# Delta attention on one Trainium2 core: block products placed in pairs on two halves of the PSUM partitions, output scaling moved to ScalarE

## The chip, the cores and the metric

The kernel runs on one core of one Trainium2 chip. The core has TensorE (PE, with its weight loads listed as PEld), VectorE (DVE), ScalarE (ACT), GpSimd (POOL) and SyncE (SP), which issues the DMAs. They run side by side and meet only through semaphores. The metric is the device time of one execution in microseconds, the median of several runs.

## The reference, cut to what matters

Input x is 4 x 1024 x 128. Four layers are added to it in turn: a gated delta-rule attention (8 heads, three delta updates in each step), a mixture of 15 experts, a decay attention and the mixture again. Only the first is touched by the change. For each head it computes, in sequence over t:

```python
q, k, v = short_conv(x @ Wq), short_conv(x @ Wk), short_conv(x @ Wv)   # 4 taps, then silu
def step(S, inp):
    S = S * exp(g_t)
    for i in range(3):
        S = S + beta_i * k_i (v_i - k_i S)       # outer product
    return S, q_t S
o = o * rsqrt(mean(o * o) + 1e-5) * rms_weight   # over the 128 columns of a head
o = (o * silu(x @ Wg)) @ Wo
```

## The kernel before, in words

`delta_attention` cuts time into chunks of 32 steps. With three updates a step, a chunk has R = 96 rows. An iteration takes SPAN = 64 steps (two chunks, `cc` 0 and 1) of all four sequences of one head, so it has U = 8 units (sequence, chunk), in two halves of HU = 4. There are 8 heads x 16 = 128 iterations' worth of work. The loop variable f runs over 142 rounds, and each round holds three stages of different chunks at once:

- the k side of iteration f: `k_tile` projects x to k and q (TensorE, lines 1100 and following), `tap0` on ScalarE (L766) and `tap1` to `tap3` on VectorE (L931) do the convolution, `ksilu` and `qsilu` on ScalarE (L798, L807) the silu. For iteration f - 1: `ktr` transposes (L1151), `ksum_` squares and sums on ScalarE (L730), `kr` scales (L738), `gram` makes k k' (L1163), `ap` masks it (L960, L964).
- the c side, iteration c = f - 11: `v_tile` and `gate_tile` (L1100), the v taps, `vsilu` (L781), `gate_` (L788), `vtr` and `vr` (L1173, L971), and the merge of the block inverses. The 96 x 96 unit-triangular system of a chunk is inverted in three diagonal blocks of 32 x 32 by GpSimd (`subst`, L701 and L704, four iterations together). Then `zm` (L1182), `wm` (L1191) and `m3` (L1199) on TensorE make the off-diagonal blocks for the eight units in PSUM tensor ZW, and `zev` (L822, L823), `w12` (L829) and `yev` (L835) on ScalarE copy them out to Zt and Yf.
- the recurrence of iteration r = f - 12 in two steps: `ks` (L1054), `rhs_` (DVE L879), `w_` (L1064), `wev` (ACT L756), `sr` (L1074), `sup` (DVE L890), and `o_` (L1089, L1090) for the output. `fo_` on GpSimd (L678, L680) makes the factor of the RMS norm, `osb_` (DVE L978) multiplies by it, `ot` transposes (L1207), `og_` (L986) gates, `out` (L1214) projects, `acc_` (L994) adds to x.

Each engine's order of work in a round is written out by hand as a list of calls at the end of its block. No engine leaves its order; a wait in one call holds all behind it. PSUM tile PP has two buffers, which tiles v0, v2, k0, k2 and v1, gate, k1, q share in turn, so a projection waits until VectorE has finished the taps of the one before it in the same buffer: for `gate_tile`

```python
need(pe, taps_ev[1], N)
```

that is the third tap of v1. Every fourth round ScalarE begins with `xt` (L841), a transposing copy of the finished diagonal blocks. `o_` already writes its four sequences' results to four groups of 32 PSUM partitions:

```python
o = o_ps[b * TC:(b + 1) * TC, cc, :]
mm(o, kqgB[N % 2][:, u, R:128], S[cc][:, b, :], start=True, stop=False)
```

A float32 matmul of the program appears as two matmuls and two weight loads in the trace, so eight units are 16.

Of the kernel before, what the change touches and what calls it, by code (L numbers as in the profile page):

```python
# [16 lines left out]
ALU = mybir.AluOpType  # L17
ACT = mybir.ActivationFunctionType
AX = mybir.AxisListType

B, T, D = 4, 1024, 128
# [3 lines left out]
R = NHH * TC  # L25
NCC = 2
SPAN = NCC * TC
U = B * NCC
KSTEPS = T // SPAN
PAD = TAPS - 1  # L30
HU = U // 2
TILE = 512
# [51 lines left out]
def need(eng, sem, n):  # L84

    if n >= 0:
        eng.wait_ge(sem, n + 1)
# [272 lines left out]
def delta_attention(nc, g):  # L360
# [7 lines left out]
    BLK = R // NHH  # L368
    with ExitStack() as ctx:
        new_sem = semaphores(nc, ctx)  # L370
        sb = lambda n, s, dt=F32: ctx.enter_context(nc.sbuf_tensor(n, s, dt))
        two = lambda n, s: [sb(f"{n}{i}", s) for i in range(2)]
# [34 lines left out]

        kqgB = two("kqgB", [128, U, 128])
        recB = two("recB", [R, U * 128 + U * TC])
        apkB, Dd = two("apkB", [64, U, 64]), two("Dd", [64, U, 64])  # L410
        Yf = two("Yf", [R, U, R])
        Zt = sb("Zt", [R, U, 64])
        vt = sb("vt", [128, U, R])
# [8 lines left out]

        pb = lambda n, s: ctx.enter_context(nc.psum_tensor(n, s, F32))
        PP, TG = [pb(f"PP{i}", [128, TILE]) for i in range(2)], pb("TG", [128, U, 128])
        ZW, RA, RB, SD = pb("ZW", [128, U, 64]), pb("RA", [128, B, 128]), pb("RB", [128, B, 128]), pb("SD", [128, TILE])
        o_ps, ot_ps = SD[:, 0:256].rearrange("p (c n) -> p c n", c=NCC), SD[:, 256:512]

        kqg_d = nc.dram_tensor("kqg_d", (SETS * KSTEPS, 128, U * 128), F32, kind="Internal").ap()
# [26 lines left out]
        def live(n):  # L455
            return 0 <= n < NS
# [4 lines left out]
        def slot(n):  # L461
            return (n // KSTEPS) % SETS * KSTEPS + n % KSTEPS
# [12 lines left out]

        def half(t, hf):
            return t[:, hf * HU:(hf + 1) * HU]

        def of_cc(t, cc):
            return t.rearrange("p (b c) n -> p b c n", c=NCC)[:, :, cc, :]  # L480
# [27 lines left out]
        def _(sp):  # L508
# [63 lines left out]
            def da_load(N):  # L572
                if not live(N):
                    return
                q = N // GROUP
                need(sp, zm_mm, N - 2)
                sp.wait_ge(preset_ev, 1)
                sp.wait_ge(st_ap[N % 2], 4 * uses(N))
                sp.dma_start(apkB[N % 2][:, :, :], apk_d[slot(N)]).then_inc(ld_da[N % 2], 16)
                sp.wait_ge(st_x[q % 2], uses(q))  # L580
                for b in range(2):
                    o = slice(BLK * b, BLK * (b + 1))
                    sp.dma_start(Dd[N % 2][o, :, o], x_d[q, lanes(N, b)].rearrange("u r c -> r u c")).then_inc(ld_da[N % 2], 16)
# [48 lines left out]
        def _(pool):  # L632
# [70 lines left out]
                    x = X[q % 2][:, j + 1:, 0:cols]  # L703
                    nc.gpsimd.tensor_tensor(x, x, t, ALU.subtract).then_inc(sub_ev, 1)  # L704

            for t in (Zt, Yf[0], Yf[1], Dd[0], Dd[1]):
                nc.gpsimd.memset(t[:, :, :], 0.0)
            nc.gpsimd.memset(S[0][:, :, :], 0.0).then_inc(preset_ev, 1)
            for f in range(NF):
# [11 lines left out]
        def _(act):  # L721
            def ksum_(N, hf):
                if not live(N):
                    return
                need(act, ktr_mm[hf], N)
                need(act, ss_ev, N - 1)
                if N >= 2:
                    act.wait_ge(st_rec[N % 2], uses(N - 2))
                for u in units_of(hf):
                    last = nc.scalar.activation(recA[N % 2][:, u * 128:(u + 1) * 128], TG[:, u, :], ACT.Square, accum_out=ksum[:, u:u + 1])  # L730
                last.then_inc(ksum_ev[hf], 1)
# [26 lines left out]
            def tap0(N, name):  # L758
                if not live(N):
                    return  # L760
                i, x = TILES[name], N // KSTEPS % 2
                src = PP[i % 2][:, 0:B * (PAD + SPAN)].rearrange("p (b t) -> p b t", b=B)
                need(act, tile_mm[i], N)
                need(act, vsilu_ev if i < 3 else qsilu_ev if i == 7 else ksilu_ev, N - 1)
                acc, w = (conv_v[:, i], tv[x][:, i, 0:1]) if i < 3 else (conv_k[:, i - 4], tk[x][:, i - 4, 0:1])
                nc.scalar.activation(acc, src[:, :, 0:SPAN], ACT.Copy, scale=w).then_inc(tap0_ev[i], 1)  # L766
# [42 lines left out]
            def mo_(N, cc):  # L809
# [3 lines left out]
                need(act, fs_ev, N - 1)  # L813
                nc.scalar.activation(osq[:, :], o_ps[:, cc, :], ACT.Square, accum_out=mo[:, cc:cc + 1]).then_inc(mo_ev[cc], 1)

            def zev(N):
                if not live(N):
                    return
                need(act, zm_mm, N)
                need(act, m3_mm, N - 1)  # L820
                act.wait_ge(preset_ev, 1)
                nc.scalar.activation(Zt[32:64, :, 0:32], ZW[0:32, :, 0:32], ACT.Copy, scale=-1.0)  # L822
                nc.scalar.activation(Zt[64:96, :, :], ZW[32:64, :, :], ACT.Copy, scale=-1.0).then_inc(zev_ev, 1)  # L823

            def w12(N):
                if not live(N):
                    return
                need(act, wm_mm, N)
                nc.scalar.activation(Yf[N % 2][32:64, :, 64:96], ZW[32:64, :, 32:64], ACT.Copy).then_inc(w12_ev, 1)  # L829

            def yev(N):
                if not live(N):
                    return
                need(act, m3_mm, N)
                nc.scalar.activation(Yf[N % 2][0:32, :, 32:96], ZW[0:32, :, :], ACT.Copy).then_inc(yev_ev, 1)  # L835

            def xt(q, k):
                if q is None or k:
# [4 lines left out]
            for f in range(NF):  # L843
                r, c = f - BACK - 1, f - BACK
                xt(*group_at(f, 2 * GROUP + 1))
                tap0(c, "v0")
                tap0(c, "v1")
                ksum_(f - 1, 1)
                ksum_(f - 1, 0)
                wev(r, 0)  # L850
                tap0(c, "v2")
                gate_(c)
                zev(c)
                tap0(f, "k1")
                mo_(r, 0)
                tap0(f, "k0")
                kr(f - 1, 0)
                vsilu(c)
                kr(f - 1, 1)
                tap0(f, "k2")  # L860
                w12(c)
                wev(r, 1)
                q2_(f - 1)
                tap0(f, "q")
                mo_(r, 1)
                yev(c)
                ksilu(f)
                qsilu(f)

        @block.vector  # L870
        def _(dve):
# [98 lines left out]
                need(dve, rk_ev, N)  # L970
                nc.vector.tensor_tensor(half(vrow[N % 2][:, :, :], hf), half(TG[0:R, :, :], hf), half(rk[:, N % RING, :], hf).unsqueeze(2).broadcast_to([R, HU, 128]), ALU.mult).then_inc(vr_ev[hf], 1)  # L971

            def osb_(N):
                if not live(N):
                    return
                need(dve, fo_ev, N)
                need(dve, ot_mm, N - 1)
                nc.vector.tensor_tensor(osb[:, :, :], o_ps, fo[:, :].unsqueeze(2).broadcast_to([128, NCC, 128]), ALU.mult).then_inc(osb_ev, 1)  # L978

            def og_(N):  # L980
                if not live(N):
                    return
# [15 lines left out]
            for f in range(NF):  # L998
                r, c = f - BACK - 1, f - BACK
                tap1(c, "v0")  # L1000
                osb_(r - 1)
                tap2(c, "v0")
                rhs_(r, 0)
                tap3(c, "v0")
                tap1(c, "v1")
                og_(r - 1)
                tap2(c, "v1")
                tap3(c, "v1")
                ss_(f - 1)
                rinv_(f - 1)  # L1010
                acc_(r - 1)
                tap1(c, "v2")
                step_(f - 1)
                tap2(c, "v2")
                tap3(c, "v2")
                sup(r, 0)
                es_(f - 1)
                tap1(f, "k1")
                tap1(f, "k0")
                tap2(f, "k0")  # L1020
                tap3(f, "k0")
                rhs_(r, 1)
                tap2(f, "k1")
                ap(f - 1, 0)
                tap3(f, "k1")
                tap1(f, "k2")
                tap2(f, "k2")
                ap(f - 1, 1)
                tap3(f, "k2")
                tap1(f, "q")  # L1030
                tap2(f, "q")
                tap3(f, "q")
                vr(c, 1)
                sup(r, 1)
                vr(c, 0)

        @block.tensor
        def _(pe):
# [137 lines left out]
            def zm(N):  # L1176
                if not live(N):
                    return
                pe.wait_ge(ld_da[N % 2], 3 * uses(N))
                need(pe, yev_ev, N - 1)  # L1180
                for u in range(U):
                    last = mm(ZW[0:64, u, :], apkB[N % 2][:, u, :], Dd[N % 2][:, u, :], start=True, stop=True)  # L1182
                last.then_inc(zm_mm, 1)

            def wm(N):
                if not live(N):
                    return
                need(pe, zev_ev, N)
                pe.wait_ge(ld_y[N % 2], 3 * uses(N))
                for u in range(U):  # L1190
                    last = mm(ZW[0:64, u, :], Zt[:, u, :], Yf[N % 2][:, u, BLK:R], start=True, stop=True)  # L1191
                last.then_inc(wm_mm, 1)

            def m3(N):
                if not live(N):
                    return
                need(pe, w12_ev, N)
                for u in range(U):
                    last = mm(ZW[0:32, u, 32:64], Zt[:, u, 0:32], Yf[N % 2][:, u, 64:96], start=True, stop=True)  # L1199
                last.then_inc(m3_mm, 1)  # L1200

            def ot(N):
# [837 lines left out]
```

## Time and profile before

| | |
|---|---|
| median of 3 runs | 3191.56 us (3190.16 to 3193.73) |
| the profiled execution's own time | 3186.49 us |
| its span | 3184.4 us |
| delta attention | from 72 us to about 2467 us of the span |
| busy share of the span | PE 94%, PEld 74%, DVE 79%, ACT 71%, POOL 62% |
| mean busy share of the DMA engines between 300 and 2310 us | 0.71 |

A row of the timeline gives the start in us, the time taken by the instructions merged into it, engine, line, operation, out<-in, shapes and count, and in brackets idle time before it with what ended it. Matmuls and weight loads overlap, so the row of 16 matmuls lasts from the first start to the last end. A row of waits gives the total in us, the number of times and the longest. A row of one source line gives the shortest, median and longest duration in ns, and the first and last start.

### The profile page before, as it was taken

Reading aid. Unit: us, or ns where it says so; the run is one execution under the profiler, and the core shown is the slowest. Engines: PE = TensorE matmul, PEld = TensorE weight load, DVE = VectorE, ACT = ScalarE, POOL = GpSimd, SP = SyncE. Lnnn points to the kernel's source line nnn. Section 1 sums busy time; section 2 is a strip of 40 time slices with the busy share of each in tenths; the row PEclk is TensorE's granted clock in tenths of the full one; section 3 lists DMA queues with packets and bytes.
Section 4 is the critical chain, followed back from the end, with each engine's and each line's share of the span. In section 5 each row is a group of like instructions: output and inputs, shape, how many; then the busy total and the mean of one; then the engine's idle time right before and its main releaser. Section 6 shows DMA issues by size and latency. Waiting matters only on the chain. (4 is left out here: it accounts for less than half of the span.)

```text
span 3184.4 us, 83423 instructions
## 1 busy us (share of the span) xinstructions
PE 2986.1 (94%) x27212; PEld 2356.1 (74%) x27212; DVE 2530.9 (79%) x5859; ACT 2250.1 (71%) x6955; POOL 1977.0 (62%) x3125
## 2 busy tenths in 40 slices
PE   5669999999999999999999999999988999867999
PEld 3458888888888888888888888888877444455444
DVE  5669999999999999999999999999855445585544
ACT  4768888888888888888888888888743444314443
POOL 1588888888888888888888888888851000100000
PEclk8779999999999999999999999999999899968999
DMA  5456777776767776767777767676732333002242
GB/s 108 121 154 167 191 180 182 172 181 170 181 172 189 177 178 174 185 167 182 174 185 178 185 171 178 176 180 168 184 96 64 129 148 130 30 3 73 108 160 113
DMA packets 588203, 482.87 MB, mean 152 GB/s; under 512 B 464784, under 2 KB 504368, under 8 KB 581632
## 3 DMA queue, kind: packets, MB, share of 16 engines
q1 hardware_dynamic: 579328, 474.39, 56.5%
q8 instruction: 223, 3.65, 0.5%
q10 hardware_dynamic: 8448, 3.15, 0.4%
q14 instruction: 204, 1.67, 0.2%
HBM read 285.53 MB, written 191.86 MB: 150 GB/s over the span
## 5 line engine op out<-in xcount | busy, mean ns | idle before, releaser
L931 DVE SCALAR_TENSOR_TENSOR conv_k<-PP,tk,conv_k 128x256 f32<-128x256 f32 x1536 | 722.7, 479 | 60.0 <-ACT conv_k L766 32.8
L704 POOL TENSOR_TENSOR X<-X,tmp 96x31 f32<-96x31 f32 (+15 forms) x992 | 534.8, 539 | 77.8
L931 DVE SCALAR_TENSOR_TENSOR conv_v<-PP,tv,conv_v 128x256 f32<-128x256 f32 x1152 | 539.3, 477 | 44.9 <-ACT conv_v L766 35.3
L701 POOL TENSOR_TENSOR tmp<-At,X 96x31 f32<-96x31 f32 (+15 forms) x992 | 486.3, 490 | 63.3 <-DMA At<-n_d 5.0
L1100 PE MATMUL PP<-xn,wk 128*128 128x268 f32 x1024 | 342.3, 418 | 38.0 <-DVE conv_k L931 26.3
L687 POOL TENSOR_TENSOR rk<-ss,half 96x8 f32<-96x8 f32 x128 | 209.1, 1634 | 175.2 <-DVE ss L899 175.2
L669 POOL TENSOR_TENSOR Sg<-S,gend 128x512 f32<-128x512 f32 x256 | 265.9, 1039 | 59.2 <-DVE S L890 59.2
L738 ACT ACTIVATE recA<-TG,es 96x128 f32<-96x128 f32 x1024 | 284.9, 368 | 5.1 <-DVE es L924 5.1
L766 ACT ACTIVATE conv_k<-PP,tk 128x256 f32<-128x256 f32 x512 | 245.3, 480 | 57.1 <-PE PP L1100 49.7
L730 ACT ACTIVATE recA<-TG 128x128 f32<-128x128 f32 x1024 | 265.5, 272 | 25.5 <-PE TG L1151 25.5
L1064 PE MATMUL RB<-rhs,Yf 96*96 96x128 f32 x2048 | 269.0, 274 | 14.5 <-DVE rhs L879 14.3
L756 ACT ACTIVATE ws<-RB 96x512 f32<-96x512 f32 x256 | 151.7, 592 | 183.0 <-PE RB L1064 180.1
L1054 PE MATMUL RA<-S,kqgB 128*96 128x128 f32 x2048 | 276.2, 278 | 1.0 <-DVE S L890 1.0
L1074 PE MATMUL RA<-ws,recB 96*128 96x128 f32 x2048 | 270.9, 275 | 0.2 <-ACT ws L756 0.2
L1064 PEld LDWEIGHTS RB<-rhs,Yf 96*96 96x96 f32 x2048 | 242.2, 163 | 36.9 <-DVE rhs L879 24.5
L1074 PEld LDWEIGHTS RA<-ws,recB 96*128 96x128 f32 x2048 | 259.0, 192 | 8.1 <-ACT ws L756 0.8
L1163 PE MATMUL TG<-kq 128*96 128x128 f32 x1888 | 245.3, 273 | 1.2 <-ACT recA L738 1.0
L1054 PEld LDWEIGHTS RA<-S,kqgB 128*96 128x96 f32 x2048 | 233.4, 163 | 13.0 <-DVE S L890 4.4
L654 POOL TENSOR_TENSOR kqgA<-kq,gdec 128x768 f32<-128x768 f32 x128 | 203.2, 1588 | 38.3 <-ACT kq L807 31.5
L1163 PEld LDWEIGHTS TG<-kq 128*96 128x96 f32 x1888 | 219.0, 163 | 2.2 <-ACT recA L738 2.2
L1100 PE MATMUL PP<-xn,wv 128*128 128x268 f32 x768 | 218.3, 391 | 2.3 <-DVE conv_k L931 2.3
L1100 PEld LDWEIGHTS PP<-xn,wk 128*128 128x128 f32 x1024 | 161.6, 197 | 69.5 <-issue 37.7
(291 smaller groups left out, 6735.0 us busy)
## 6 DMA issues: line engine op xcount, KB each, us to landing
kqg_d<-kqgA SPq DMA_DIRECT2D x128, 512.0 KB, 6.4
kqgB<-kqg_d SPq DMA_DIRECT2D x128, 512.0 KB, 4.5
rec_d<-recA SPq DMA_DIRECT2D x128, 480.0 KB, 3.4
recB<-rec_d SPq DMA_DIRECT2D x128, 480.0 KB, 6.0
f1gates<-f1gates_d SPq DMA_DIRECT2D x24, 1024.0 KB, 6.5
f2gates<-f2gates_d SPq DMA_DIRECT2D x24, 1024.0 KB, 6.8
gdec<-gdec_d SPq DMA_DIRECT2D x128, 128.0 KB, 5.8
apk_d<-apkA SPq DMA_DIRECT2D x128, 128.0 KB, 3.3
```

Of the source, the lines that this page charges most:

```text
L669: nc.gpsimd.tensor_tensor(Sg[:, :, :], S[cc][:, :, :], d.broadcast_to([128, B, 128]), ALU.mult).then_inc(sg_ev[cc], 1)
L701: nc.gpsimd.tensor_tensor(t, At[q % 2][:, j, j + 1:].unsqueeze(2).broadcast_to(sh), X[q % 2][:, j, 0:cols].unsqueeze(1).broadcast_to(sh), ...
L704: nc.gpsimd.tensor_tensor(x, x, t, ALU.subtract).then_inc(sub_ev, 1)
L730: last = nc.scalar.activation(recA[N % 2][:, u * 128:(u + 1) * 128], TG[:, u, :], ACT.Square, accum_out=ksum[:, u:u + 1])
L738: last = nc.scalar.activation(recA[N % 2][0:R, u * 128:(u + 1) * 128], TG[0:R, u, :], ACT.Copy, scale=es[:, u, TC - 1:TC])
L766: nc.scalar.activation(acc, src[:, :, 0:SPAN], ACT.Copy, scale=w).then_inc(tap0_ev[i], 1)
L931: return nc.vector.scalar_tensor_tensor(acc, src[:, :, j:j + SPAN], w[:, j:j + 1], acc, ALU.mult, ALU.add)
L1054: last = mm(RA[0:R, b, :], kqgB[N % 2][:, b * NCC + cc, 0:R], S[cc][:, b, :], start=True, stop=True)
L1064: last = mm(RB[0:R, b, :], Yf[N % 2][:, b * NCC + cc, :], rhs[:, b, :], start=True, stop=True)
L1074: last = mm(RA[:, b, :], recB[N % 2][:, u * 128:(u + 1) * 128], ws[cc][:, b, :], start=True, stop=True)
L1100: mm(out, w, x, start=True, stop=True).then_inc(tile_mm[i], 1)
L1163: last = mm(gram_bank(N, hf)[0:R, u % HU, :], kq[N % 2][:, u, 0:R], kq[N % 2][:, u, :], start=True, stop=True)
```

## The change

- `zm`, `wm` and `m3` write the products of units 0 to 3 to PSUM partitions 0 to 63 and those of units 4 to 7 to partitions 64 to 127 of ZW, which is half as long, and go through the units in the order 0, 4, 1, 5, 2, 6, 3, 7.
- apkB and Dd have 96 partitions in place of 64, the last 32 are zero, so `zm` contracts over 96 rows. GpSimd clears apkB too at the start. `m3` takes all 64 columns of Zt as weights in place of 32.
- `zev`, `w12` and `yev` take two copies, one from each half, where they took one: 4, 2 and 2 instructions in place of 2, 1 and 1.
- `osb_` moves from VectorE (one instruction over both chunks, after `tap1` of v0) to ScalarE (one Copy with a scale for each chunk, after `tap0` of v1 and ahead of `ksum_`).

```diff
-        apkB, Dd = two("apkB", [64, U, 64]), two("Dd", [64, U, 64])
+        apkB, Dd = two("apkB", [R, U, 64]), two("Dd", [R, U, 64])
-        ZW, RA, RB, SD = pb("ZW", [128, U, 64]), ...
+        ZW, RA, RB, SD = pb("ZW", [128, HU, 64]), ...
+        def paired():
+            return (HU * p + i for i in range(HU) for p in range(2))
+        def spot(u, lo, hi):
+            return ZW[64 * (u // HU):64 * (u // HU) + 64, u % HU, lo:hi]
-            for t in (Zt, Yf[0], Yf[1], Dd[0], Dd[1]):
+            for t in (Zt, Yf[0], Yf[1], Dd[0], Dd[1], apkB[0], apkB[1]):
                 nc.gpsimd.memset(t[:, :, :], 0.0)
...
+            def osb_(N):                      # ScalarE
+                need(act, fo_ev, N)
+                need(act, ot_mm, N - 1)
+                for cc in range(NCC):
+                    last = nc.scalar.activation(osb[:, cc, :], o_ps[:, cc, :], ACT.Copy, scale=fo[:, cc:cc + 1])
+                last.then_inc(osb_ev, 1)
             def zev(N):
-                nc.scalar.activation(Zt[32:64, :, 0:32], ZW[0:32, :, 0:32], ACT.Copy, scale=-1.0)
-                nc.scalar.activation(Zt[64:96, :, :], ZW[32:64, :, :], ACT.Copy, scale=-1.0).then_inc(zev_ev, 1)
+                for p in range(2):
+                    nc.scalar.activation(half(Zt[32:64, :, 0:32], p), ZW[64 * p:64 * p + 32, :, 0:32], ACT.Copy, scale=-1.0)
+                    last = nc.scalar.activation(half(Zt[64:96, :, :], p), ZW[64 * p + 32:64 * p + 64, :, :], ACT.Copy, scale=-1.0)
+                last.then_inc(zev_ev, 1)
             def w12(N):
-                nc.scalar.activation(Yf[N % 2][32:64, :, 64:96], ZW[32:64, :, 32:64], ACT.Copy).then_inc(w12_ev, 1)
+                for p in range(2):
+                    last = nc.scalar.activation(half(Yf[N % 2][32:64, :, 64:96], p), ZW[64 * p + 32:64 * p + 64, :, 32:64], ACT.Copy)
+                last.then_inc(w12_ev, 1)
             def yev(N):
-                nc.scalar.activation(Yf[N % 2][0:32, :, 32:96], ZW[0:32, :, :], ACT.Copy).then_inc(yev_ev, 1)
+                for p in range(2):
+                    last = nc.scalar.activation(half(Yf[N % 2][0:32, :, 32:96], p), ZW[64 * p:64 * p + 32, :, :], ACT.Copy)
+                last.then_inc(yev_ev, 1)
...
                 tap0(c, "v1")
+                osb_(r - 1)
                 ksum_(f - 1, 1)
...
-            def osb_(N):                      # VectorE
-                nc.vector.tensor_tensor(osb[:, :, :], o_ps, fo[:, :].unsqueeze(2).broadcast_to([128, NCC, 128]), ALU.mult).then_inc(osb_ev, 1)
                 tap1(c, "v0")
-                osb_(r - 1)
                 tap2(c, "v0")
...
-                for u in range(U):
-                    last = mm(ZW[0:64, u, :], apkB[N % 2][:, u, :], Dd[N % 2][:, u, :], start=True, stop=True)
+                for u in paired():
+                    last = mm(spot(u, 0, 64), apkB[N % 2][:, u, :], Dd[N % 2][:, u, :], start=True, stop=True)
...
-                for u in range(U):
-                    last = mm(ZW[0:64, u, :], Zt[:, u, :], Yf[N % 2][:, u, BLK:R], start=True, stop=True)
+                for u in paired():
+                    last = mm(spot(u, 0, 64), Zt[:, u, :], Yf[N % 2][:, u, BLK:R], start=True, stop=True)
...
-                for u in range(U):
-                    last = mm(ZW[0:32, u, 32:64], Zt[:, u, 0:32], Yf[N % 2][:, u, 64:96], start=True, stop=True)
+                for u in paired():
+                    last = mm(spot(u, 32, 64), Zt[:, u, :], Yf[N % 2][:, u, 64:96], start=True, stop=True)
```

## Rows read from the trace of the kernel before

**Rows 1.** Busy time of each engine between 300 and 2310 us (PE, PEld, DVE, ACT, POOL, clock, DMA).

```profile
300.00:2310.00 2010.00, 1999.97 (x20403) 1737.17 (x20400) 1842.20 (x4293) 1718.32 (x5558) 1704.50 (x2726) 1.00 0.71 178
```

**Rows 2.** Waits between 1000 and 2000 us: who for whom, total us, times, longest.

```profile
ACT ws L756 <- PE RB L1064: 58.9, 56, 1.2
...
PEld ZW L1191 <- issue: 19.9, 56, 0.4
...
DVE osb L978 <- POOL fo L680: 4.6, 14, 0.4
```

**Rows 3.** Timeline, ScalarE: the gate copy of three rounds in a row.

```profile
1489.65 0.38 ACT L788 ACTIVATE gate<-PP 128x256 f32<-128x256 f32 x1 [0.37 <-PE PP L1100]
...
1507.17 0.38 ACT L788 ACTIVATE gate<-PP 128x256 f32<-128x256 f32 x1 [0.37 <-PE PP L1100]
...
1525.44 0.38 ACT L788 ACTIVATE gate<-PP 128x256 f32<-128x256 f32 x1 [0.72 <-PE PP L1100]
```

**Rows 4.** Source line 822 up to 2312 us: one instruction a round.

```profile
L822 ACT ACTIVATE Zt<-ZW x119: 372/373/374, 216.4 to 2304.8; 32x256 f32<-32x256 f32 x119
```

**Rows 5.** Timeline, TensorE, one round.

```profile
1503.42 1.14 PE L1182 MATMUL ZW<-Dd,apkB 64*64 64x64 f32 x16
...
1508.41 0.45 PE L1089 MATMUL SD<-S,kqgB 128*32 128x128 f32 x8
1508.65 0.42 PE L1090 MATMUL SD<-ws,recB 96*32 96x128 f32 x8
...
1509.66 1.15 PE L1191 MATMUL ZW<-Yf,Zt 96*64 96x64 f32 x16
...
1512.56 0.62 PE L1100 MATMUL PP<-xn,wk 128*128 128x268 f32 x2
1513.02 1.04 PE L1064 MATMUL RB<-rhs,Yf 96*96 96x128 f32 x8
...
1514.77 0.62 PE L1100 MATMUL PP<-xn,wk 128*128 128x268 f32 x2
1515.32 0.45 PE L1089 MATMUL SD<-S,kqgB 128*32 128x128 f32 x8
...
1515.78 0.67 PE L1199 MATMUL ZW<-Yf,Zt 96*32 96x32 f32 x16
```

**Rows 6.** Timeline, ScalarE, the same round and the start of the next.

```profile
1507.58 0.37 ACT L822 ACTIVATE Zt<-ZW 32x256 f32<-32x256 f32 x1
1507.96 0.59 ACT L823 ACTIVATE Zt<-ZW 32x512 f32<-32x512 f32 x1
...
1514.76 0.84 ACT L747 ACTIVATE q<-ss 32x2 f32<-32x2 f32 x4
1515.62 0.47 ACT L766 ACTIVATE conv_k<-PP,tk 128x256 f32<-128x256 f32 x1
...
1518.36 2.01 ACT L841 ACTIVATE At<-X 96x1024 f32<-96x1024 f32 x1
...
1520.28 0.81 ACT L766 ACTIVATE conv_v<-PP,tv 128x256 f32<-128x256 f32 x2
```

**Rows 7.** Timeline, VectorE, end of that round and start of the next.

```profile
1510.28 1.52 DVE L931 SCALAR_TENSOR_TENSOR conv_k<-PP,tk,conv_k 128x256 f32<-128x256 f32 x3 [0.27 <-ACT conv_k L766]
...
1519.00 0.68 DVE L971 TENSOR_TENSOR vrow<-TG,rk 96x512 f32<-96x512 f32 x1
1520.76 0.48 DVE L931 SCALAR_TENSOR_TENSOR conv_v<-PP,tv,conv_v 128x256 f32<-128x256 f32 x1 [1.09 <-ACT conv_v L766]
1521.16 0.41 DVE L978 TENSOR_TENSOR osb<-SD,fo 128x256 f32<-128x256 f32 x1
...
1523.66 0.99 DVE L931 SCALAR_TENSOR_TENSOR conv_v<-PP,tv,conv_v 128x256 f32<-128x256 f32 x2
```

**Rows 8.** Timeline, GpSimd: after the clearing at the start, and the norm's factor.

```profile
83.02 1.58 POOL L654 TENSOR_TENSOR kqgA<-kq,gdec 128x768 f32<-128x768 f32 x1 [7.41 <-ACT kq L807]
...
1537.93 0.70 POOL L680 TENSOR_TENSOR fo<-fo,minus_half 128x2 f32<-128x2 f32 x1
```

More of the change, by code:

```diff
@@ L424, in delta_attention @@
         PP, TG = [pb(f"PP{i}", [128, TILE]) for i in range(2)], pb("TG", [128, U, 128])
-        ZW, RA, RB, SD = pb("ZW", [128, U, 64]), pb("RA", [128, B, 128]), pb("RB", [128, B, 128]), pb("SD", [128, TILE])
+        ZW, RA, RB, SD = pb("ZW", [128, HU, 64]), pb("RA", [128, B, 128]), pb("RB", [128, B, 128]), pb("SD", [128, TILE])
         o_ps, ot_ps = SD[:, 0:256].rearrange("p (c n) -> p c n", c=NCC), SD[:, 256:512]
@@ L578, in da_load @@
                 sp.wait_ge(st_ap[N % 2], 4 * uses(N))
-                sp.dma_start(apkB[N % 2][:, :, :], apk_d[slot(N)]).then_inc(ld_da[N % 2], 16)
+                sp.dma_start(apkB[N % 2][0:64, :, :], apk_d[slot(N)]).then_inc(ld_da[N % 2], 16)
                 sp.wait_ge(st_x[q % 2], uses(q))
@@ L814, in mo_ @@
                 nc.scalar.activation(osq[:, :], o_ps[:, cc, :], ACT.Square, accum_out=mo[:, cc:cc + 1]).then_inc(mo_ev[cc], 1)
+            def osb_(N):
+                if not live(N):
+                    return
+                need(act, fo_ev, N)
[3 more added lines that the diff above has]
+                last.then_inc(osb_ev, 1)
             def zev(N):
@@ L971, in vr @@
                 nc.vector.tensor_tensor(half(vrow[N % 2][:, :, :], hf), half(TG[0:R, :, :], hf), half(rk[:, N % RING, :], hf).unsqueeze(2).broadcast_to([R, HU, 128]), ALU.mult).then_inc(vr_ev[hf], 1)
-            def osb_(N):
[L974 to L977, printed above, removed]
-                nc.vector.tensor_tensor(osb[:, :, :], o_ps, fo[:, :].unsqueeze(2).broadcast_to([128, NCC, 128]), ALU.mult).then_inc(osb_ev, 1)
             def og_(N):
```

## The prediction

> **What bounds the kernel now.** First the page's share of busy time, which names TensorE; then the same by stage, since the change touches only delta attention. Between 300 and 2310 us TensorE is busy for 1999.97 of 2010 us [rows 1], at a granted clock of 1.00, and the others for 85 to 92%. Next the waits in the middle of that stretch: ScalarE waits for TensorE (58.9 us in 56 rounds at `wev`), while TensorE's loads wait mainly on "issue", which is no other engine [rows 2]. So an ordinary round is TensorE's own work. Its length is read from one instruction that comes once a round: 1489.65 to 1507.17 is 17.52 us, 1507.17 to 1525.44 is 18.27 us [rows 3]. The longer one is the round with `xt`, every fourth; there VectorE waits 1.09 us for ScalarE's tap of v0 [rows 7], and the gate copy waits 0.72 us in place of 0.37. Four rounds take 3 x 17.52 + 18.27 = 70.83 us. From 216.4 to 2304.8 us there are 119 rounds [rows 4], 29 such groups; the last ten, without k side, come after.
>
> **TensorE's part.** `zm` takes 1.14 us, of which 0.22 is the latency of the last matmul: 0.92/15 = 0.061 us from start to start; `wm` is the same at 1.15 [rows 5]. It contracts over 96 rows where `zm` has 64, so the padding costs nothing. Do halves run side by side? `o_` says so: its 16 matmuls of 128 columns, on four groups of 32 partitions, start within 1508.41 to 1508.80 (1508.65 + 0.42 less a latency of 0.27), 0.026 us each, while `w_` on full width needs (1.04 - 0.27)/7 = 0.11 each [rows 5]. Two halves then give a pair each 0.061 us: 8 x 0.061 = 0.49 in place of 0.95, a gain of 0.46 us for `zm` and 0.46 for `wm`. `m3` has 16 matmuls in 0.67 - 0.20 = 0.47 us, 0.031 each, but gets 64 weight columns, and nothing with 64 columns steps faster than 0.061; a pair at that is 0.49, so no gain. It now also differs in tile width from `o_` ahead of it, where before it joined on without a gap. The price of a change of width: L1100 to L1064, both wide, is 0.46 us, L1100 to L1089, wide to narrow, 0.55 [rows 5], so 0.09; the "issue" waits reach 0.4 [rows 2]. I take 0.10, nearer TensorE's own starts, and 0.09 to 0.4 for the range. TensorE's round: 17.52 - 0.46 - 0.46 + 0.02 + 0.10 = 16.72.
>
> The Trainium skill, "TensorEngine Tiling (Array Packing)", section "Tiling Modes", says that a change of tiling mode drains the array; it gives no price, and the 0.09 above agrees in kind.
>
> **ScalarE's part.** A copy of 32 partitions takes 0.37 us for 256 elements and 0.59 for 512 [rows 6], so 0.16 + 0.00083 n, which gives 0.27 for 128; four copies of two elements take 0.84, 0.21 each, a little above the line's foot, so I take 0.29 for 128. Bounds from both sides: no fixed cost (a half costs half), or a half costs a whole. `zev`: two of 128 and two of 256 are 2 x (0.29 + 0.385) = 1.35 against 0.99, +0.36 (0 to 0.97). `w12`: +0.19 (0 to 0.40). `yev`: its second half runs into the next instruction, +0.17 (0 to 0.49). `osb_`: 2 x 0.26 = 0.52. All 1.24 us a round, while ScalarE's idle time is (2010 - 1718.32)/2010 x 17.71 = 2.57 us [rows 1]. It fits, but not where it likes: the order is fixed, so I follow the chain that now closes through three engines.
>
> **The chain.** From the gate copy on, ScalarE goes through its list to the tap of q: 1507.17 to 1515.62, 8.45 us [rows 3, 6], in which it waits 0.36 for TensorE's k tiles, of which about 0.30 would go: 8.15. `zev` and `w12` lie in it: 8.70. From the tap of q VectorE does three taps of q, `vr`, `sup`, `vr`, and the first tap of v0: 1515.62 to 1519.00 + 0.60 = 3.98, less 0.22 idle before `sup`: 3.76. From there to the end of the third tap of v1: 1520.76 to 1523.66 + 0.99 = 3.89 [rows 7]. Here `osb_` goes: first to second tap was 0.73 with it, and is 0.52 without, since three dependent taps take 1.52 and 0.48 of that is the last one [rows 7]; so 3.68, not 0.41 less. Then the gate tile on TensorE and the gate copy again: 1524.65 to 1525.44, 0.79. Sum 8.70 + 3.76 + 3.68 + 0.79 = 16.93 us. That is above TensorE's 16.72, so **an ordinary round ends at 16.93**, and VectorE and ScalarE together take 0.2 of what TensorE frees.
>
> The `xt` round: 8.70 + (1515.62 to 1520.28 = 4.66, + 0.17 for `yev`) + 0.48 to VectorE + 3.68 + 0.79 = 18.48, against 18.27: it gets longer, since it was bound by ScalarE already. `osb_` on ScalarE lies outside both chains, behind v1's tap; ScalarE's 1.2 us wait at `wev` covers it.
>
> Four rounds: 3 x 16.93 + 18.48 = 69.27, against 70.83: 1.56 saved, x 29 = 45 us. The last ten rounds, bound by the recurrence, I count at nothing (at most 0.3 each). The two more clearings of 0.5 us at the start lie ahead of 7.41 us in which GpSimd waits [rows 8]: nothing. ZW at half length may shift the PSUM tensors behind it; no row prices that, I take nothing. The profiled execution (3186.5, span 3184.4) would take 3141; it lies 5 us below the median of the runs, so the forecast is **3146 us**, 1.4% less.
>
> **The wait added.** `osb_` on ScalarE waits for `fo_`. Behind it stand `ksum_` (for VectorE's `ss_`, then GpSimd's `rk_`) and `wev`. In the round after `xt`, GpSimd is late: `fo_` ends at 1537.93 + 0.70, 13.19 us after the gate copy of 1525.44 [rows 3, 8], and VectorE then waits 0.33 (4.6 us in 14 times [rows 2]). In the new round ScalarE reaches `osb_` about 12.5 us after the gate copy, so it stalls 0.7 us. Then 0.52 + 2.2 for `ksum_` leads to 16.0; `wev` could start at 16.93 - 1.32 = 15.6 and with v2's tap takes 0.96: 16.96, just in time for the gate copy at 16.93. So nothing, but without margin.
>
> **Rivals.**
> 1. *The halves do not overlap* (slower). For it: `o_` has 32 weight columns and these have 64; nothing before shows two 64-column tiles side by side. Against: starts of `o_`, and loads that are hidden behind matmuls of the same rows in `zm` and `wm`. Place: `m3`, 16 x 0.061 = 0.98 against 0.47, + 0.10; TensorE's round 18.13. Four: 3 x 18.13 + 18.48 = 72.87, +2.04 x 29 = +59: **3251**. It decides from a round of (70.83 - 18.48)/3 = 17.45 on, that is when the 24 pairs take more than 17.45 - 16.72 = 0.73 us above my 1.47, 0.092 us a pair. Chance 0.09. The Trainium skill, "TensorE: Matmul & The Clock Gate", Part 3, says that a weight load overlaps matmuls in flight only when the row group differs, which is not so in a pair; by that rule this rival is the result. The trace speaks against the rule: `zm` steps at 0.061 us with one row group throughout.
> 2. *Half a copy costs a whole* (slower): 8.15 + 0.97 + 0.40 + 3.76 + 3.68 + 0.79 = 17.75; `xt` round 9.52 + 5.15 + 0.48 + 3.68 + 0.79 = 19.62; +2.04 a group: **3251**. The 0.37 against 0.59 speaks against it. Chance 0.04.
> 3. *`osb_` stalls ScalarE for good*: the 0.7 us and some 0.4 in the round after are not covered; 1.1 a group off: 0.46 x 29 = 13: **3178**. Chance 0.15.
> 4. *Only TensorE bounds*: copies nearer their lower bound; 3 x 16.72 + 18.27 = 68.43, 2.40 x 29 = 70: **3122**. Chance 0.11.
> 5. Gains and additions cancel: 3192, chance 0.04.
>
> **Numbers.** The forecast's case has 0.57. A measurement of this kernel tells about 0.2% (6 us) from no change. Faster 0.57 + 0.15 + 0.11 = 0.83, same 0.04, slower 0.09 + 0.04 = 0.13. The range from 3116 to 3180 takes in cases 3 and 4 and leaves out 0.17.
>
> **What would show it.** Right: ordinary rounds of 16.9 us and `xt` rounds of 18.5 by the gate copy; `zm` and `wm` at 0.7 us a row, `m3` at 0.7; TensorE idle 0.2 us a round at the gate tile; four 32-partition copies of 0.29 a round; ScalarE waiting for `fo_` in one round of four. Wrong: `zm` still at 1.14; ordinary rounds of 16.7 or over 17.2; an `xt` round below 18.2.

## The result, and the profile after

The changed kernel takes 3139.82 us, median of 4 runs (3133.41 to 3144.35), against 3190.86 us (4 runs, 3185.2 to 3193.73) for the kernel before on the same chip: ratio 0.984, 95% interval 0.9827 to 0.9852. It is faster, 6 us below the forecast and inside the range. The profiled execution took 3139.86 us, with a span of 3138.0.

The page of the changed kernel, busy time of each engine:

```profile
PE 2919.0 (93%) x27212; PEld 2241.5 (71%) x27212; DVE 2486.9 (79%) x5731; ACT 2346.9 (75%) x7723; POOL 1977.9 (63%) x3127
```

TensorE issues as many matmuls as before (x27212) and is 67 us less busy; ScalarE has 768 instructions more and is 97 us busier. The share by engine would still name TensorE. The window that answers to [rows 1]:

```profile
300.00:2270.00 1970.00, 1941.94 (x20489) 1636.51 (x20488) 1807.41 (x4192) 1803.62 (x6248) 1713.78 (x2742) 1.00 0.73 182
```

TensorE now idles 28 us of 1970, where it was 10 of 2010; ScalarE idles 8% where it was 15%. The granted clock is 1.00 in both. Waits from 1000 to 2000 us, for [rows 2] (waiting engine, tile, line, releaser: total us, times, longest):

```profile
DVE conv_k L953 <- ACT conv_k L772: 35.2, 87, 0.5
...
ACT osb L828 <- POOL fo L686: 20.3, 29, 0.8
...
PEld SD L1103 <- ACT ws L762: 20.2, 57, 0.4
...
ACT ws L762 <- PE RB L1078: 7.8, 14, 0.6
...
PEld TG L1177 <- ACT recA L744: 2.6, 14, 0.2
```

ScalarE's wait for TensorE at `wev` fell from 58.9 to 7.8 us: TensorE is no longer the slower of the two by a whole microsecond a round. VectorE's wait for ScalarE's taps of k and q grew from 13.5 to 35.2 us. ScalarE's wait for `fo_` is new: the prediction expected it in one round of four, and it comes in two (29 times in 58 rounds). New too is a small one, `gram` for the scaled k rows, of which more below; the list leaves out short idle stretches and shows this one in 14 rounds only, where the timeline has it in all.

The gate copy, one a round, as in [rows 3]:

```profile
1458.18 0.38 ACT L794 ACTIVATE gate<-PP 128x256 f32<-128x256 f32 x1 [0.35 <-PE PP L1114]
...
1475.06 0.38 ACT L794 ACTIVATE gate<-PP 128x256 f32<-128x256 f32 x1 [0.37 <-PE PP L1114]
...
1493.37 0.38 ACT L794 ACTIVATE gate<-PP 128x256 f32<-128x256 f32 x1 [0.72 <-PE PP L1114]
...
1510.25 0.38 ACT L794 ACTIVATE gate<-PP 128x256 f32<-128x256 f32 x1 [0.18 <-PE PP L1114]
...
1527.17 0.38 ACT L794 ACTIVATE gate<-PP 128x256 f32<-128x256 f32 x1 [0.35 <-PE PP L1114]
```

The rounds are 16.88, 18.31 (with `xt`), 16.88 and 16.92 us; 69.00 us for four, mean over the middle of the run, against 70.84: 1.84 saved. (Round lengths below are read in the same way.) Where the 46.4 us of span went, from one source line:

```profile
L794 ACT ACTIVATE gate<-PP x128: 383/383/384, 217.3 to 2393.8; 128x256 f32<-128x256 f32 x128
```

```profile
L788 ACT ACTIVATE gate<-PP x128: 383/384/384, 216.0 to 2442.4; 128x256 f32<-128x256 f32 x128
```

The second is the kernel before. The first gate copy comes 1.3 us later, the 127 rounds take 2176.5 us in place of 2226.4 (49.9 less), and the rest of the span, from the last gate copy on, is 744.2 in place of 742.0. By the gate copies, the first 116 rounds (29 groups) take 2000.0 us in place of 2053.0, which is 53.0 less, and the last eleven 176.6 in place of 173.5, 3.1 more. Most of these last rounds are shorter than before (14.95 in place of 15.13), but three of the last ten take 16.5 to 17.8 us, where one did (16.7).

TensorE in the round from 1493.37 on, for [rows 5]:

```profile
1495.86 0.69 PE L1205 MATMUL ZW<-Yf,Zt 96*64 96x64 f32 x16
1496.47 1.11 PE L1068 MATMUL RA<-S,kqgB 128*96 128x128 f32 x8
1497.51 1.11 PE L1177 MATMUL TG<-kq 128*96 128x128 f32 x8
1498.46 0.62 PE L1114 MATMUL PP<-xn,wk 128*128 128x268 f32 x2
...
1501.46 0.42 PE L1104 MATMUL SD<-ws,recB 96*32 96x128 f32 x8
1501.82 0.66 PE L1213 MATMUL ZW<-Yf,Zt 96*64 96x32 f32 x16
1502.40 1.08 PE L1187 MATMUL TG<-ident,vt 128*96 128x128 f32 x8
...
1506.96 0.69 PE L1196 MATMUL ZW<-Dd,apkB 96*64 96x64 f32 x16
1507.58 0.44 PE L1221 MATMUL SD<-ident,osb 128*128 128x128 f32 x2
```

`zm` and `wm` went from 1.14 and 1.15 to 0.69. From the start of `zm` to the start of `ot` it is 0.62, where it was 1.08; the same for `wm`. `m3` is unchanged at 0.66, as forecast, but starts 0.36 us after the second half of `o_` where it was 0.22. The starts add up to 17.52 - 0.46 - 0.46 - 0.01 + 0.13 = 16.72 us for TensorE's own work, the forecast's value. Yet the round is 16.88. The difference lies at `gram` (L1177): it starts 1.04 us after `ks` (L1068), where it was 0.95, and the k2 tile starts 0.95 us after `gram`, where it was 0.87. Averaged over the ordinary rounds between 1000 and 2000 us that is 0.08 and 0.08 us. All other steps from start to start, those of `zm`, `wm` and `m3` aside, are as in the kernel before, to 0.01 us; so the move of the PSUM tensors behind ZW cost it nothing.

ScalarE in the same round, for [rows 6]:

```profile
1493.77 0.27 ACT L838 ACTIVATE Zt<-ZW 32x128 f32<-32x128 f32 x1
1494.05 0.37 ACT L839 ACTIVATE Zt<-ZW 32x256 f32<-32x256 f32 x1
1494.44 0.27 ACT L838 ACTIVATE Zt<-ZW 32x128 f32<-32x128 f32 x1
1494.72 0.38 ACT L839 ACTIVATE Zt<-ZW 32x256 f32<-32x256 f32 x1
...
1495.97 0.47 ACT L772 ACTIVATE conv_k<-PP,tk 128x256 f32<-128x256 f32 x1
1496.34 1.12 ACT L744 ACTIVATE recA<-TG,es 96x128 f32<-96x128 f32 x4
...
1501.99 0.47 ACT L772 ACTIVATE conv_k<-PP,tk 128x256 f32<-128x256 f32 x1
...
1506.57 0.62 ACT L828 ACTIVATE osb<-SD,fo 128x128 f32<-128x128 f32 x2 [0.78 <-POOL fo L686]
```

The four copies of `kr` end at 1496.34 + 1.12 = 1497.46, and `gram` starts at 1497.51. In the kernel before the same place had room:

```profile
1492.25 0.47 ACT L766 ACTIVATE conv_k<-PP,tk 128x256 f32<-128x256 f32 x1 [0.23 <-PE PP L1100]
1492.62 1.11 ACT L738 ACTIVATE recA<-TG,es 96x128 f32<-96x128 f32 x4
...
1493.22 1.11 PE L1054 MATMUL RA<-S,kqgB 128*96 128x128 f32 x8
1494.17 1.04 PE L1163 MATMUL TG<-kq 128*96 128x128 f32 x8
1495.04 0.62 PE L1100 MATMUL PP<-xn,wk 128*128 128x268 f32 x2
```

There `kr` ended at 1493.73 and `gram` followed at 1494.17, 0.44 us later. The k0 projection (at 1491.49 before, 1495.21 after) starts both paths: TensorE goes on through `wm` and `ks` to `gram`, ScalarE through the tap of k0 and `kr`. From k0 to `gram` TensorE needed 2.68 us before; without 0.46 of `wm` it would be 2.22, now ScalarE's path holds it at 2.30, 0.05 us after the last copy of `kr`. So the room had been 0.38 us. With the 0.08 that `gram` itself then takes longer to the next tile, that costs 0.16 us a round (0.20 in the round of 16.92).

### The profile page after: what moved, and what is told of

It reads as the page before. It is cut to its first block and busy times, and to the rows that moved or that the text cites. A ratio compares the mean times of both kernels' runs of the same rounds, so it can differ in the third digit from the quotient of the medians.

```text
span 3138.0 us, 84065 instructions
## 1 busy us (share of the span) xinstructions
PE 2919.0 (93%) x27212; PEld 2241.5 (71%) x27212; DVE 2486.9 (79%) x5731; ACT 2346.9 (75%) x7723; POOL 1977.9 (63%) x3127
## 5 line engine op out<-in xcount | busy, mean ns | idle before, releaser
L1068 PE MATMUL RA<-S,kqgB 128*96 128x128 f32 x2048 | 276.1, 278 | 1.0 <-DVE S L912 1.0
L1177 PE MATMUL TG<-kq 128*96 128x128 f32 x1888 | 254.2, 277 | 1.7 <-ACT recA L744 1.5
L736 ACT ACTIVATION_READ_ACCUMULATOR recA<-TG 128x1 f32 x1024 | 245.8, 243 | 0.0
L1068 PEld LDWEIGHTS RA<-S,kqgB 128*96 128x96 f32 x2048 | 233.6, 163 | 12.9 <-DVE S L912 4.1
L1177 PEld LDWEIGHTS TG<-kq 128*96 128x96 f32 x1888 | 215.6, 163 | 19.7 <-ACT recA L744 7.9
```

The lines of the kernel that those rows point to most:

```text
L1068: last = mm(RA[0:R, b, :], kqgB[N % 2][:, b * NCC + cc, 0:R], S[cc][:, b, :], start=True, stop=True)
L1177: last = mm(gram_bank(N, hf)[0:R, u % HU, :], kq[N % 2][:, u, 0:R], kq[N % 2][:, u, :], start=True, stop=True)
```

## The experiments

All times beside a run's are of the kernel before on the same chip, in the same session; one run each where no interval is given.

**Only ScalarE's side.** The kernel before, with the split copies and `osb_` on ScalarE; the products stay on partitions 0 to 63, one unit after the other:

```diff
-                nc.scalar.activation(Zt[64:96, :, :], ZW[32:64, :, :], ACT.Copy, scale=-1.0).then_inc(zev_ev, 1)
+                for p in range(2):
+                    nc.scalar.activation(half(Zt[32:64, :, 0:32], p), half(ZW[0:32, :, 0:32], p), ACT.Copy, scale=-1.0)
+                    last = nc.scalar.activation(half(Zt[64:96, :, :], p), half(ZW[32:64, :, :], p), ACT.Copy, scale=-1.0)
```

> The kernel before with ScalarE's and VectorE's side of the change alone: osb_ on ScalarE, and zev, w12 and yev as two copies of half the units each; the products still lie on partitions 0 to 63 and come in single file. Theory (a round is as long as its longest closed chain, and TensorE's own 17.52 us is the longest here): zm and wm rows still 1.14 us, ordinary rounds 17.52 us, xt rounds 18.3 to 18.5, a group of four 70.9 to 71.1 against 70.84, so 0 to +8 us in all. Rival (ScalarE's added 1.24 us a round is paid in full): ordinary rounds above 18 us, over +100 us. Rival (the gain of the change comes from relieving VectorE): ordinary rounds shorter than 17.52.

Measured: 3186.36 us (10 runs, 3183.88 to 3189.27) against 3187.65, ratio 0.9991 (0.9982 to 1.0001). Rounds 17.52 three times, 18.14 with `xt`; 70.69 for four, so the `xt` round and the group lie below what was expected. So 1.2 us a round more on ScalarE is free as long as TensorE's 17.52 holds. The `xt` round got 0.14 shorter, since VectorE lost `osb_` (3.68 us from v0's first tap to v1's third, where it was 3.89), and of the longer ScalarE list only 0.05 us showed ahead of q's tap and next to nothing behind it.

**Only the pairs.** The changed kernel with `osb_` back on VectorE after `tap1` of v0:

```diff
-                osb_(r - 1)
                 ksum_(f - 1, 1)
...
                 tap1(c, "v0")
+                osb_(r - 1)
```

> The changed kernel with osb_ put back on VectorE after the first tap of v0. Theory (chain through q's tap, VectorE's taps of v0 and v1 and the gate tile, which osb_ lengthens by 0.21 us): ordinary rounds between 16.88 (where the chain through wev and o_ binds) and 17.15, xt rounds 18.5, a group 69.2 to 69.9 against 69.00, +6 to +26 us against the changed kernel; no wait of ScalarE for the norm's factor. Rival (TensorE alone bounds): 69.0, no difference. Rival (the 0.6 to 0.8 us waits for the factor cost something): shorter than 69.0.

Measured: 3171.76 us against 3187.65, rounds 17.55 (right after `xt`), 17.05, 17.04, 18.54; 70.15 for four, above what was expected. Two ordinary rounds and the `xt` round are longer than in the changed kernel by 0.12 to 0.24: `osb_` makes VectorE's chain of taps 0.21 longer, as in the prediction. The miss is the round after `xt`. VectorE's timeline in it:

```profile
1456.19 0.42 DVE L990 TENSOR_TENSOR osb<-SD,fo 128x256 f32<-128x256 f32 x1 [0.40 <-POOL fo L686]
```

`osb_` waits 0.40 us for `fo_` between two taps of v0, and all taps up to v1's third, then the gate tile, stand behind it. So the two halves of the change do not add up: 0.15 us a group for ScalarE's side alone, 0.69 for the pairs alone, 1.84 together. Each alone leaves the other's loop in force.

**Halves without pairs.** The products on two halves, in the order 0 to 7:

```diff
-            return (HU * p + i for i in range(HU) for p in range(2))
+            return range(U)
```

> The changed kernel with the units in their plain order 0 to 7: all eight matmuls of the lower half, then all eight of the upper. Theory A (each half of the columns works off its own queue, fed far ahead, as in o_, where four matmuls in a row go to one group): zm's first to last start stays near 0.5 us and rounds at 16.9. Theory B (overlap only between neighbours in the order): 16 x 0.058 = 0.93 us again for zm and wm and as much for m3, TensorE's round 18.1, over +100 us against the changed kernel, so slower than before.

Measured: 3208.01 us against 3187.65; rounds 17.54 three times, 18.60; 71.2. TensorE's timeline:

```profile
1482.36 0.97 PE L1205 MATMUL ZW<-Yf,Zt 96*64 96x64 f32 x16
...
1488.44 0.91 PE L1213 MATMUL ZW<-Yf,Zt 96*64 96x32 f32 x16
```

Less the last one's latency, sixteen matmuls take 0.75 us: more than 0.47 in pairs, less than 0.92 on one half, so neither of the two theories on record. The records show a few of the upper half running beside the last of the lower one, where the halves change, and no overlap elsewhere. `m3`, which gained nothing from the pairs, takes 0.25 more than in the changed kernel (0.91 in place of 0.66). So the interleaved order gives the gain: the same instructions on the same halves, in plain order, are 20 us slower than the kernel before (one run).

**The tap of q ahead of `q2_`**, to shorten ScalarE's list to the tap by the 0.84 us of `q2_`:

```diff
-                q2_(f - 1)
                 tap0(f, "q")
+                q2_(f - 1)
```

> The changed kernel with q2_ (four small copies, 0.86 us) behind the tap of q on ScalarE instead of ahead of it. Theory (two chains near each other: 16.88 through wev of step 1, o_ and TensorE to the gate tile; 16.93 through q's tap): the second gets 0.86 us of room, the first does not, so ordinary rounds are 16.88 all three, xt rounds unchanged (their chain holds q2_ in either place), group 68.9 to 69.0, under -3 us. Rival (the forecast's chain through q's tap is the bound): ordinary rounds 16.7, group 68.4, -17 us.

Measured: 3169.04 us against 3187.65, rounds 17.10 three times, 18.77; 70.09: longer than the changed kernel where it should have been no longer. ScalarE's timeline:

```profile
1486.82 0.47 ACT L772 ACTIVATE conv_k<-PP,tk 128x256 f32<-128x256 f32 x1 [0.20 <-PE PP L1114]
1487.31 0.84 ACT L753 ACTIVATE q<-ss 32x2 f32<-32x2 f32 x4
```

The tap now waits 0.20 us for its tile. After it `q2_` starts at +0.49; in the changed kernel `mo_` starts 0.37 us after the tap, 0.10 before it ends. `mo_`'s two instructions start 0.29 apart, not 0.16. The `xt` round, which is ScalarE's whole list, grew by 0.47 us: 0.20 is the wait, and the other 0.27 the order alone. The silu of k comes that much later too, and TensorE's transposes wait for it (24.3 us in 58 times).

**`m3` with 32 weight columns.** Written to the same places, so that a weight load has half the columns:

```diff
-                    last = mm(spot(u, 32, 64), Zt[:, u, :], Yf[N % 2][:, u, 64:96], start=True, stop=True)
+                    last = mm(spot(u, 32, 64)[0:32], Zt[:, u, 0:32], Yf[N % 2][:, u, 64:96], start=True, stop=True)
```

> The changed kernel with m3 taking 32 weight columns and writing 32 partitions in each half, the tile width of o_ ahead of it. TensorE's own work should fall by 0.25 us in m3 and by the 0.08 us that the first matmuls now take longer, 0.33 in all, to 16.4 us a round. Theory (three closed chains of nearly one length: through wev of step 1 and o_, 16.88; through q's tap and VectorE, 16.94; all of ScalarE's list with xt, 18.30): only the first contains m3, so ordinary rounds go to the second, 16.88 to 16.94, and the group stays at 68.9 to 69.0. Rival (TensorE's own work is what bounds the changed kernel): ordinary rounds 16.55, group 68.0, -29 us.

> The same kernel as x_m3_narrow, timed: rounds as there (group 68.90), so 3 us off 29 groups and about 3 us off the ten last rounds (14.6 in place of 14.9 us), 3134 us, ratio to the kernel before 0.982.

Measured: 3130.07 us against 3190.96; timed again on another chip, 3130.3 us (5 runs, 3128.68 to 3134.31) against 3191.09, ratio 0.9813 (0.9799 to 0.9826). Rounds 16.83, 16.93, 16.82, 18.32; 68.90 and 68.96 for four. TensorE's timeline of the timed one:

```profile
1481.47 0.42 PE L1104 MATMUL SD<-ws,recB 96*32 96x128 f32 x8
1481.69 0.44 PE L1213 MATMUL ZW<-Yf,Zt 96*32 96x32 f32 x16
1482.06 1.08 PE L1187 MATMUL TG<-ident,vt 128*96 128x128 f32 x8
```

and two of its waits:

```profile
PEld PP L1114 <- DVE conv_v L953: 22.5, 73, 0.5
...
PEld TG L1165 <- ACT kq L804: 19.9, 58, 0.4
```

`m3` takes 0.44 in place of 0.66 and joins on to `o_` after 0.22 us again, since both have 32 columns; from there to `vtr` it is 0.59 in place of 0.94, 0.35 us less for TensorE. Of that the round keeps 0.05. If nothing else held it, the first loop would now allow 16.53. What holds the round are the waits of `ktr` for the silu of k and of `gate_tile` for v1's taps, that is ScalarE's list and VectorE's taps, the chain of the prediction. In two of the three ordinary rounds its steps are 8.64, 3.71 to 3.74, 3.67 and 0.79 us, 16.81 to 16.84 together, so it lies 0.05 us under the first loop. It is still the fastest version here that computes everything, some 9 us below the changed kernel (the two ratios' intervals, up to 0.9826 and from 0.9827, just miss each other). Only 1.4 us of it lies in the first 116 rounds. The last eleven take 171.0 us in place of 176.6: the short ones take 14.60 in place of 14.95, but how many longer ones come between them changes from one execution to the next (the first run of this same kernel has 174.1), so how much of the 9 us is the edit's is not shown.

**`wev` before `w12`.** TensorE's load for `o_` seemed to wait 20.2 us for ScalarE's `wev` (the waits above), 0.35 a round:

```diff
-                w12(c)
                 wev(r, 1)
+                w12(c)
```

> The changed kernel with wev of step 1 ahead of w12 on ScalarE. Theory: the chain through o_ loses w12's 0.57 us (16.3), the copy after a tap overlaps it by 0.1 us more, and so the chain through q's tap and the xt round get 0.1 us shorter: ordinary rounds 16.82, xt rounds 18.2, group 68.6 to 68.8, -5 to -10 us. The wait of TensorE's o_ of step 1 for ScalarE (20.2 us in 57 rounds) goes. Rival (that wait is the bound alone): ordinary rounds 16.55.

> Both edits: wev of step 1 ahead of w12, and m3 with 32 weight columns. Theory: as wev alone, since the chain through q's tap holds neither m3 nor w12's place: ordinary rounds 16.82, xt 18.2, group 68.6 to 68.8; against the kernel before -58 to -62 us, ratio 0.981. Rival (the edits add up on TensorE): ordinary rounds 16.4, group 67.4, -45 us against the changed kernel.

Measured: 3145.93 us against 3190.96, 69.07 for four. Together with the narrow `m3`: 3133.23 us (5 runs, 3128.23 to 3136.18), ratio 0.9817 (0.9804 to 0.9831), 69.05. No gain, a miss. The waits of the first of these:

```profile
PEld SD L1103 <- issue: 41.2, 116, 0.4
```

The wait for `ws` is gone, and "issue" at the same line has grown by the same 20.6 us. In the kernel before, both of a round's gaps in front of `o_` had stood under "issue":

```profile
PEld SD L1089 <- issue: 40.1, 113, 0.4
```

The gap of 0.35 us in front of `o_` is there whatever ScalarE does, and for `wev` the profile had only named what happened to come last. The edit even cost a little: `wev` now has to wait for `w_`, a wait that `w12` had filled, and the path from the gate copy to q's tap is 8.69 us in both runs, where it was 8.63. That puts the chain of the prediction at 16.86 to 16.90, which is where two of the three ordinary rounds of the second run lie (16.86 and 16.89).

**`vr` between q's taps**, with both edits above, so that VectorE gets to v0 sooner:

```diff
                 tap2(f, "q")
-                tap3(f, "q")
                 vr(c, 1)
+                tap3(f, "q")
```

> As x_wev_narrow, and VectorE's vr of the second half between the second and third tap of q, so that the 0.12 us that a dependent tap waits is filled. Theory (chain through q's tap and VectorE binds ordinary and, with the whole of ScalarE's list, not xt rounds): ordinary rounds 0.12 us shorter than in x_wev_narrow, xt rounds the same, group -0.36, -10 us. Rival: no change or longer, because q's third tap is now 0.6 us later for the v1 tile, which waits for it.

Measured: 3138.86 us against 3190.96; 69.35 for four, 0.3 more where 0.36 less was hoped. The waits:

```profile
PEld PP L1114 <- DVE conv_k L953: 29.2, 54, 0.5
```

v1's projection waits for the third tap of q, since the two share a PSUM buffer. The rival was right.

**Half of the copies.** This one leaves out the second copy in `zev`, `w12` and `yev`, so that units 4 to 7 are built from old blocks; ScalarE's list is 0.9 us shorter ahead of q's tap, and 1.3 in all.

```diff
-                for p in range(2):
+                for p in range(1):
```

> The changed kernel with the second copy of zev, w12 and yev left out: Zt and Yf keep old values for units 4 to 7, so four heads' chunks are computed from wrong blocks. It prices ScalarE's copies: 0.65 + 0.28 + 0.37 = 1.3 us a round less. Theory (ordinary rounds: the k0 tile, ScalarE's tap of it, four kr copies and gram on one side, q's tap and VectorE on the other; xt rounds: the whole of ScalarE's list): the chain through q loses 0.93 (16.0), xt rounds 1.3 (17.0); then TensorE's own 16.72 plus the 0.16 it waits for kr before gram, which lies behind the k0 tile and not behind the copies, stays: ordinary 16.88, xt 17.3 to 17.6, group 68.0. Rival (the zev copies themselves delay kr): ordinary rounds 16.72.

Measured: 3114.69 us against 3191.09; rounds 16.88, 16.94, 16.88, 17.71; 68.45 for four. ScalarE and TensorE in one round:

```profile
1483.84 0.47 ACT L772 ACTIVATE conv_k<-PP,tk 128x256 f32<-128x256 f32 x1 [0.23 <-PE PP L1114]
1484.21 1.12 ACT L744 ACTIVATE recA<-TG,es 96x128 f32<-96x128 f32 x4
...
1485.38 1.11 PE L1177 MATMUL TG<-kq 128*96 128x128 f32 x8
```

This is the run that settles the ordinary round. From the gate copy to q's tap it is 8.35 us, only 0.28 less than in the changed kernel, since ScalarE now waits for tiles instead. With ScalarE 1.3 us lighter two of the three ordinary rounds stay at 16.88, and TensorE's starts at `gram` are those of the changed kernel (1.03 and 0.95). `kr` ends at 1485.33 and `gram` starts at 1485.38, as in the changed kernel; ahead of them ScalarE waits for the k0 tile. So neither the new copies nor my chain sets it, but k0 tile, tap, `kr`, `gram`. The `xt` round, in contrast, falls by 0.6, a little less than expected.

**`mo_` behind `kr`**, to see whether ScalarE's work ahead of `kr` is what delays `gram`:

```diff
-                mo_(r, 0)
                 tap0(f, "k0")
                 kr(f - 1, 0)
+                mo_(r, 0)
```

> The changed kernel with mo_ of step 0 (0.25 us on ScalarE) behind the four kr copies of the first half instead of ahead of the tap of k0. Theory (gram waits for kr, kr for the tap of k0, and that for TensorE's k0 tile, which ScalarE has been waiting 0.12 us for): kr and gram come no earlier, ordinary rounds at least 16.88; mo_ no longer fills the time in which ScalarE waits, so the chain through q's tap is 0.15 to 0.25 us longer: ordinary rounds 16.95 to 17.15, xt rounds 18.5, group 69.4 to 70.0. Rival (kr is late because ScalarE is busy from the gate copy on): ordinary rounds 0.16 us shorter, group 68.5.

Measured: 3162.95 us against 3191.09; rounds 17.08 three times, 18.57; 69.84, as expected. ScalarE's timeline:

```profile
1472.63 0.38 ACT L794 ACTIVATE gate<-PP 128x256 f32<-128x256 f32 x1 [0.37 <-PE PP L1114]
...
1475.23 0.47 ACT L772 ACTIVATE conv_k<-PP,tk 128x256 f32<-128x256 f32 x1 [0.38 <-PE PP L1114]
...
1481.53 0.47 ACT L772 ACTIVATE conv_k<-PP,tk 128x256 f32<-128x256 f32 x1
```

`kr` comes no earlier, since its tap now waits 0.38 us for the k0 tile, and `gram` still costs its 0.16 (1.03 and 0.95 from start to start), though it is no longer in the list of waits. So it is the tile and not `mo_` that holds `kr`. From the gate copy to q's tap it is 8.90 us, against 1475.06 to 1483.69 = 8.63 in the changed kernel: 0.27 more on my chain, 0.20 more a round. That would put the chain less than 0.1 us under the first loop, as the narrow `m3` did. But this run alone does not show it, for TensorE has the 0.20 in another place, at the second `gram`:

```profile
1478.18 1.04 PE L1078 MATMUL RB<-rhs,Yf 96*96 96x128 f32 x8
1479.14 1.11 PE L1177 MATMUL TG<-kq 128*96 128x128 f32 x8
```

That is 0.96 us where it was 0.87, and the next two starts are 0.07 and 0.05 later: `mo_` delays the second four copies of `kr` as well, and the second `gram` now waits for them. Both paths come to 17.08 within 0.02 us.

## Why the prediction was right

The sum was made against one execution: 3186.49 - 45 = 3141, measured 3139.86. Term by term:

- **TensorE's part** was right: pairs at 8 x 0.061 us, `zm` and `wm` 0.46 less each, `m3` unchanged, the change of width 0.13 us where 0.10 was taken (0.09 to 0.4). TensorE's own round 16.72, as forecast. Rival 1, that halves do not overlap, fell with 0.69 against 1.14. So did, here, the rule of the Trainium skill in "TensorE: Matmul & The Clock Gate", Part 3, that a weight load overlaps only matmuls of another row group: all eight units use the same rows, and the two of a pair start 7 ns apart, a pair every 58 ns, while the loads run beside matmuls in flight (the last row of this document).
- **ScalarE's part** was right for `zev` (four copies spaced 1.35, as forecast), `w12` (0.27 a copy) and `osb_` (two Copies spaced 0.52 to the next instruction). `yev` cost 0.04 in place of 0.17 in the `xt` round. Rival 2 is out with 0.27 against 0.37.
- **The chain** holds step by step: gate copy to q's tap 8.63 (8.70); from there to v0's first tap on VectorE 3.74 (3.76); to the end of v1's third tap 3.72 (3.68); to the gate copy 0.80 (0.79). Its sum is 16.89, and 16.93 was forecast. A closed path adds up to the round whatever binds it, waits included, so the sum alone shows nothing; what the chain needs by itself is shown by the narrow `m3`, 16.81 to 16.84. VectorE's rows for it:

```profile
1505.73 0.99 DVE L953 SCALAR_TENSOR_TENSOR conv_v<-PP,tv,conv_v 128x256 f32<-128x256 f32 x2
...
1508.46 0.99 DVE L953 SCALAR_TENSOR_TENSOR conv_v<-PP,tv,conv_v 128x256 f32<-128x256 f32 x2
```

- **The step that was missing**: "That is above TensorE's 16.72, so an ordinary round ends at 16.93" names the wrong binder. TensorE closes a shorter loop of its own through k0's tap, `kr` and `gram`, 16.72 + 0.16 = 16.88. I had looked for waits that existed before; this one had 0.38 us of room (`gram` came 0.44 us after `kr`, and follows it by 0.05 at least), less than the 0.46 taken out of `wm` ahead of it. The sign named for the chain, TensorE idle 0.2 us a round at the gate tile, did not appear: the starts around that tile are 0.43 us apart as before. The two loops agree within 0.05 us, so the ordinary round came out right by luck, through the wrong loop. The half-copies run tells them apart.
- **The step that was mis-sized** is the `xt` round: 18.48 forecast, 18.30 measured, from 0.07 in ScalarE's list and 0.13 in `yev`. With 0.03 in each ordinary round that makes 1.84 saved a group, not 1.56, so 53 us over 29 groups where I had 45. The last eleven rounds (+3.1 us), the stretch after the last gate copy (+2.2) and the start (+1.3) gave some of it back, and 46.4 remained. I had counted these at nothing. In the runs above the last eleven take 170 to 184 us, the stretch after them 738.6 to 747.7 and the start 215.0 to 218.2, and two executions of one kernel differ by 3.1, 1.5 and 1.2, so the three additions are no more than the scatter between runs. That the total came within 2 us of the forecast is in this part luck too.
- **The wait for `fo_`** was there as forecast: 0.78 us in the round after `xt` (0.7 forecast), and 0.6 in the next one, which I had not expected. It is covered: both rounds keep 16.88 and 16.92, and the gate copy still waits for its tile after it. Rival 3 is out. In the `xt` round TensorE waits for `osb_` as well, 0.5 us ahead of `ot`; that round's chain runs through the taps and is 18.30 without it. What I undervalued is the other side of this move. On VectorE the same wait would have stood in the chain, as the run with pairs only shows: about 1.15 of the 1.84 us a group need the move of `osb_`.
- **Rival 4**, TensorE alone, at 16.72: out by 0.16 us a round, and only by that.

## What to carry to other kernels

When a change takes time out of the binding engine, list every loop that closes through it, with the room that each has now, and compare the room with what is taken out ahead of it: a wait that the profile before does not show is one whose room was not yet used up. Measure both halves of a change alone before crediting either; here they gave 0.15 and 0.69 us a group alone, and 1.84 together. And before moving work to end a wait, see whether the gap stays with another name when its supposed cause is early.

## What the runs showed of the hardware

- Two streams of 64-column weight tiles on the two halves of the result's partitions overlap fully only if they alternate: the sixteen matmuls in the trace of eight float32 products take 0.47 us alternating, 0.75 with the halves one after the other, 0.92 on one half, at a granted clock of 1.00. The loads run beside the matmuls; TensorE's weight loads in the changed kernel:

```profile
1495.86 0.55 PEld L1205 LDWEIGHTS ZW<-Yf,Zt 96*64 96x64 f32 x16 [0.35 <-issue]
```

- Where a narrow weight tile follows one of another width there is a stretch without a load: 0.35 us in front of `o_` (32 columns after 128) and `wm` (64 after 128), 0.2 in front of `m3` (64 after 32) and of `zm` (64 after 128). At `m3` 0.13 us of it showed between the starts of the matmuls, and with 32 columns in `m3` the stretch was gone from the waits. The profile may put such a gap down to another engine's last event.
- On ScalarE, most instructions on 96 or 128 partitions start about 0.10 us before the one ahead has ended (the tap and `kr` above: 0.37 from start to start, 0.47 long). The 32-partition copies of `zev`, `w12` and `q2_` do not, neither among themselves (0.27 long and 0.28 apart, 1493.77 and 1494.05) nor with what stands before and behind them. It is not the partition count alone: `yev`, on 32 partitions too, overlaps its neighbours by 0.09 to 0.11 us. What decides it is not shown. Moving the four of `q2_` behind the tap of q cost 0.27 us a round by the order alone.
